# A graph kernel's edge scatters, moved: two ranges ahead of the first node tables, 22 beside the first convolution's count matrices, none beside the second's strips

## The chip, the cores and the metric

One core of one Trainium2 chip. The time is the device time of one launch in microseconds (us). Lower is better.

## The reference

Two layers over one graph of N = 6250 nodes (128 features) and E = 200000 edges; edges come sorted by destination, and the low destinations are far denser than the high ones.

```
h = relu(layernorm(x)); x = x + conv(relu(conv(h, W1, b1)), W2, b2)      # conv: segment_sum(h[src] * norm, dst)
h = relu(layernorm(x)); msg = relu(concat(h[src], edge_attr) @ W1 + b1)  # one message per edge
agg = segment_sum(msg, dst) / max(count, 1)
x = x + relu(concat(h, agg) @ W2 + b2)
```

## The kernel before, in words

Five engines run their own instruction streams: PE (TensorE), DVE (VectorE), ACT (ScalarE), POOL (GpSimd) and SP (SyncE). They meet at semaphores only. All loops of the stages below are written out, but for the message stage's.

1. **Setup.** DVE and PE rank the edges of 24 ranges (`RANGES`, each 32 columns of 128 edges): `slot_of_edge` says where each edge's row of 34 words goes, so that a range comes out sorted by source. POOL gathers, among other things, the 21 blocks of edges (L715) from which the first convolution's counts are built.
2. **Node tables.** For each of 13 groups of nodes the four compute engines make the table of `h @ W` and its three bf16 parts.
3. **First convolution.** The matrix of edge counts (source by target) is built in 24 strips of 256 targets. A strip has 32 windows: DVE makes one-hots for 8 visits at a time (L1753, L1757), PE multiplies them (`build_window`, L908), ACT takes the counts out of PSUM (L1206, semaphore `C["evacuated"]`) and stores the strip to DRAM. Between windows PE applies the strip before: 49 blocks by 3 parts, 147 matmuls of 256 columns (`apply`, L920). Strips 0 to 9 have windows with many visits, 10 to 15 have two visits of 392 columns, 16 to 23 two of 196.
4. **Node tables of the second convolution**, and then its 24 strips: the counts come back from DRAM (3136 KB a strip, two buffers), PE applies them with 147 matmuls a strip, and DVE adds the sum to `agg` (`add_strip`, L1766, semaphore `strip_added`).
5. **Third tables and messages.** The scattered rows (`permuted`) are loaded in order and joined with gathered rows, until the end of the run.

A few edges past the strips (one turn: 32 gathers on POOL, L638) are handled inside each convolution, on PE after strip 2's first segment and after strip 4.

The change is about POOL's 768 scatters. `scatter(r, pace)` issues the 32 indirect DMAs of range r; each writes 128 rows of 136 bytes. Halfway through a range it waits until the one before has landed and stages the next range's rows. The `pace` hook waits ahead of each scatter. `beside_windows(i)` lets scatter i go when ACT has taken out i * 768 / (number of scatters) windows; `beside_strips(i)` lets it go when a given strip has been added. Nothing needs the scattered rows before stage 5, and no engine waits for POOL there before that. POOL executes in order, so whatever stands behind a scatter on POOL waits for it: in stage 3 the turn's gathers stand ahead of the scatters, in stage 4 as well.

Of the kernel before, what the change touches and what calls it, by code (L numbers as in the profile page):

```python
# [13 lines left out]
P = 128  # L14
# [9 lines left out]
TC = 4  # L24
CE = TC * P
SLOTS = 8
# [15 lines left out]
STRIPS = 24  # L42
# [4 lines left out]
UNIT = 8  # L47
# [14 lines left out]
RANGES = 24  # L62
RT = 32
# [21 lines left out]
MESSAGE_CHUNKS = (PAIRS - 1) * PAIR_CHUNKS + LAST_CHUNKS  # L85
PAIR_STEPS = PAIR_UNITS + 2
PREPARED_AT = (5, DU + 8)
PACED = (16, 8)
KEYS = W * SB


# [18 lines left out]
assert DT % (SLOTS * TC) == 0 and LAST_CHUNKS % SLOTS == 0 and RANGES % 2 == 0 and DU % 2 == 0 and sum(UNIT_TILES) == SB and RT % 2 == 0  # L110
assert DT * P >= RANGE_ROWS
assert all((b - a) * SB <= 512 for a, b in TILE_GROUPS) and RT * P < OWN_EDGE and RANGES % RANK_BATCH == 0
assert sum(PACED) == RANGES and P % UNIT == 0


def build(nc, t, out):
    with ExitStack() as ctx:
# [300 lines left out]
        def tables_stored(engine, n):  # L418

            for q in range(2):  # L420
                engine.wait_ge(tab_stored[q], 16 * ((NG + 1 - q) // 2) * (n + 1))
# [206 lines left out]
        def _(pool):  # L628
            def gather_turn(e, n, i, pace=lambda k: None):
                for h in range(2):  # L630
                    pool.wait_ge(e["idx_" + "ab"[h]], i * 16 + 16)
                    for k in range(HALF * TC):
                        s, j = h * HALF + k // TC, k % TC
                        if j == 0:
                            pool.wait_ge(e["added"], i * SLOTS + s + 1)
                            pool.sem_inc(held["pool"])
                        pace(h * HALF * TC + k)
                        nc.gpsimd.indirect_dma_start(  # L638
                            rows[:, s, j * D:(j + 1) * D], None, tables[n],
                            bass.IndirectOffsetOnAxis(ap=idx[:, h, k:k + 1], axis=0),  # L640
                        ).then_inc(e["gathered"][s // e["apart"]], 16)

            def gather(e, n, first, turns):
                with pool.Fori(first, turns) as i:
                    gather_turn(e, n, i)
# [21 lines left out]
            def stage(r):  # L667
                pool.dma_start(edge_rows_of[:, r % 2], t["edge_cols"][:, r * RT:(r + 1) * RT].rearrange("p t c -> p (t c)")
                               ).then_inc(rows_staged[r % 2], 16)

            def scatter(r, pace=lambda k: None):

                pool.wait_ge(ranked, r + 1)
                pool.wait_ge(rows_staged[r % 2], 16 * (r // 2 + 1))
                for k in range(RT):
                    if k == RT // 2 and 1 <= r < RANGES - 1:
                        pool.wait_ge(scattered[(r - 1) % 2], ((r - 1) // 2 + 1) * RT * 16)
                        stage(r + 1)
                    pace(k)
                    nc.gpsimd.indirect_dma_start(  # L680
                        permuted, bass.IndirectOffsetOnAxis(ap=slot_of_edge[:, r * RT + k:r * RT + k + 1], axis=0),
                        edge_rows_of[:, r % 2, k * ROW_WORDS:(k + 1) * ROW_WORDS], None,
                    ).then_inc(scattered[r % 2], 16)

            def beside_windows(i):

                pool.wait_ge(C["evacuated"], BANKS + i * NW // (PACED[0] * RT))

            def beside_strips(i):

                strip = i * STRIPS // (SLOTS * TC + PACED[1] * RT)
                pool.wait_ge(strip_added[strip % 2], STRIPS // 2 + strip // 2 + 1)
                pool.sem_inc(held["pool"])

# [19 lines left out]
            for b in range(VB):  # L714
                nc.gpsimd.indirect_dma_start(  # L715
                    visit_edges[:, b].rearrange("p k e -> p (k e)"), None, t["edge_rows"],
                    bass.IndirectOffsetOnAxis(ap=visit_row[:, b:b + 1], axis=0)).then_inc(visits_gathered, 16)
            pool.wait_ge(blanked, 16 * (RANGES + 1))
            for n in range(2):
                tables_stored(pool, n)  # L720
                pool.wait_ge(G["own"], NG * (n + 1))
                pool.wait_ge(G["part"], NG * PARTS * (n + 1))
                e = shared_passes[n]
                if n == 0:
                    pool.wait_ge(edges_read, 2)
                    turns = pool.value_load(turns_i[0:1, 1:2], min_val=1, max_val=TURNS)
                    gather_turn(e, n, 0)
                    for r in range(PACED[0]):
                        scatter(r, lambda k: beside_windows(r * RT + k))
                    with pool.If(turns > 1):  # L730
                        gather(e, n, 1, turns)
                    pool.wait_ge(flag_ready, 2)
                    flagged = pool.value_load(flag[0:1, 0:1], min_val=0, max_val=1)
                else:
                    with pool.If(flagged < 1):
                        turns = pool.value_load(turns_i[0:1, 1:2], min_val=1, max_val=TURNS)
                        gather_turn(e, n, 0, beside_strips)
                        for r in range(PACED[0], RANGES):
                            scatter(r, lambda k: beside_strips(SLOTS * TC + (r - PACED[0]) * RT + k))
                        with pool.If(turns > 1):  # L740
                            gather(e, n, 1, turns)
                with pool.If(flagged > 0):
                    gather(full_passes[n], n, 0, TURNS)
                    if n:
                        for r in range(PACED[0], RANGES):
                            scatter(r)
            tables_stored(pool, 2)
            with pool.If(flagged < 1):
                gather_messages()
# [601 lines left out]
        def _(dve):  # L1351
# [335 lines left out]
            def edge_turn(e, i, first, messages=False):  # L1687

                bases = [None] * SLOTS
                if not e["every"]:  # L1690

                    _, bases = nc.values_load_multi_w_load_instructions(
                        chunk_window[0:1, 0, bass.ds(turn_at(first, i) * SLOTS, SLOTS)], engines=[mybir.EngineType.DVE],
                        min_val=0, max_val=NP - P)
# [191 lines left out]
            def messages_mixed():  # L1886
# [56 lines left out]
                def pair_of(k, chunks, last):  # L1943
                    added = 0
                    for u in range(PAIR_STEPS):
                        c = chunk_of(u, chunks)
                        if u == DU + 2:
                            add_range(k, 0, added)
                        if u < PAIR_UNITS:
                            source(k, u)  # L1950
                        if c is not None and (not last or c + 1 < chunks):
                            hot(k, c + 1)
                        if 1 <= u <= PAIR_UNITS:
                            target(k, u - 1)
                        if c is not None:
                            if c % SLOTS == 0:
                                _, bases = nc.values_load_multi_w_load_instructions(
                                    chunk_window[0:1, 0, bass.ds(k * PAIR_CHUNKS + (FIRST_TURN * SLOTS + c), SLOTS)],
                                    engines=[mybir.EngineType.DVE], min_val=0, max_val=NP - P)
                            add(k, c, bases[c % SLOTS])  # L1960
                            added = c + 1
                            if not last or c + 2 < chunks:
                                products_in(k, c + 2)
                        if u == PREPARED_AT[0]:
                            prepare(k, 1)
                        if u == PREPARED_AT[1] and not last:
                            dve.wait_ge(B["target"], k * PAIR_UNITS + DU)
                            prepare(k + 1, 0)
                    add_range(k, 1, added)
# [90 lines left out]
```

## Time and profile before

| | before |
|---|---|
| time, median of 3 runs | 3475.75 us (3471.35 to 3476.24) |
| span of the profiled execution | 3499.7 us |
| PE busy (matmul) | 2746.7 us, 78% |
| DVE busy | 1592.3 us, 45% |
| ACT busy | 1071.7 us, 31% |
| POOL busy | 1876.6 us, 54% |
| POOL scatters (L680) | 768, 871.7 us, 1135 ns each |
| queue 8, kind "instruction" | 103 packets, 1.69 MB |

The page gives the profiled execution's span alone, from the first to the last instruction; it is 24 us above the median of the runs shown. Busy time is time in which an engine executes; waits and the issuing of DMAs by SP and ACT are not in it. An indirect DMA on POOL counts as busy for as long as POOL works on its descriptors.

### The profile page before, as it was taken

Reading aid. Unit: us, or ns where it says so; the run is one execution under the profiler, and the core shown is the slowest. Engines: PE = TensorE matmul, PEld = TensorE weight load, DVE = VectorE, ACT = ScalarE, POOL = GpSimd, SP = SyncE. Lnnn points to the kernel's source line nnn. Section 1 sums busy time; section 2 is a strip of 40 time slices with the busy share of each in tenths; the row PEclk is TensorE's granted clock in tenths of the full one; section 3 lists DMA queues with packets and bytes.
Section 4 is the critical chain, followed back from the end, with each engine's and each line's share of the span. In section 5 each row is a group of like instructions: output and inputs, shape, how many; then the busy total and the mean of one; then the engine's idle time right before and its main releaser. Section 6 shows DMA issues by size and latency. Waiting matters only on the chain.

```text
span 3499.7 us, 54147 instructions
## 1 busy us (share of the span) xinstructions
PE 2746.7 (78%) x18926; PEld 2159.2 (62%) x18927; DVE 1592.3 (45%) x3094; ACT 1071.7 (31%) x3149; POOL 1876.6 (54%) x1751
## 2 busy tenths in 40 slices
PE   2755697889947765787878647998998989888987
PEld 0114486777736654565656536777777777777766
DVE  7988985766623433000000253444444444444436
ACT  6504234556625533000000012333333333333321
POOL 3750767778866732534445134565565555555660
PEclk9995989999968977878888768999999999999989
DMA  9012122323322323433434232323233233332321
GB/s 358 28 35 76 34 83 96 130 98 128 147 85 94 133 97 97 159 124 132 163 125 163 91 98 69 94 90 101 90 95 92 86 104 92 89 92 88 105 73 45
DMA packets 127284, 365.86 MB, mean 105 GB/s; under 512 B 36226, under 2 KB 79591, under 8 KB 120599
## 3 DMA queue, kind: packets, MB, share of 16 engines
q10 hardware_dynamic: 21792, 186.56, 13.8%
q0 software_dynamic: 58928, 89.45, 10.0%
q1 hardware_dynamic: 46377, 87.47, 7.1%
q8 instruction: 103, 1.69, 0.2%
q14 instruction: 84, 0.69, 0.1%
HBM read 230.80 MB, written 132.55 MB: 104 GB/s over the span
## 4 chain that ended last, share of the span: by engine, by line
PE 62%; DVE 11%; issue 10%; another core or an unknown queue 8%; ACT 3%; POOL 2%; DMA 1%; ACTq 1%; DVEq 0%; SPq 0%; POOLq 0%
PE ps_feat L920 12%; PE ps_node L920 11%; PE ps_extra L1069 7%; PE ps_sum L1032 4%; PE pre_banks L908 3%; PE pre_banks L1023 3%; PE ps_feat L1057 3%; PE ps_feat L1053 3%; PE ps_sum L1053 2%; PE ps_sum L1057 2%; PE ps_node L1053 2%; PE ps_node L1057 2%; POOL region_b L705 2%; DVE region_c L1757 2%
## 5 line engine op out<-in xcount | busy, mean ns | idle before, releaser
L680 POOL DMA_INDIRECT permuted<-rows_or_lows,slot_of_edge x768 | 871.7, 1135 | 528.3 <-DVE agg L1766 222.9
L662 POOL DMA_INDIRECT rows<-table,region_a x800 | 786.5, 983 | 685.7 <-issue 210.5
L920 PE MATMUL ps_feat<-region_a,region_b 128*128 128x256 bf16 x3528 | 506.9, 290 | 71.4 <-issue 70.8
L920 PE MATMUL ps_node<-region_a,region_b 128*128 128x256 bf16 x3528 | 513.6, 290 | 60.6 <-issue 57.6
L920 PEld LDWEIGHTS ps_feat<-region_a,region_b 128*128 128x128 bf16 x3528 | 359.3, 103 | 156.5 <-issue 97.4
L920 PEld LDWEIGHTS ps_node<-region_a,region_b 128*128 128x128 bf16 x3528 | 358.2, 103 | 148.7 <-issue 86.9
L1069 PE MATMUL ps_extra<-region_b 128*128 128x128 f32 x2352 | 335.0, 284 | 86.4 <-ACT region_b L1299 48.0
L1069 PEld LDWEIGHTS ps_extra<-region_b 128*128 128x128 f32 x2352 | 302.0, 199 | 92.6 <-issue 72.1
L1757 DVE TENSOR_TENSOR region_c<-iota_key,region_c 128x1568 bf16<-128x1568 f16 (+1 forms) x324 | 353.2, 1090 | 0.0
L1933 DVE TENSOR_TENSOR region_b<-consts,region_a 128x512 f32<-128x512 f32 x336 | 208.2, 620 | 186.9 <-PE ps_extra L1069 97.6
L1928 DVE TENSOR_SCALAR region_b<-rows_or_lows,consts 128x512 f32<-128x512 bf16 x336 | 159.8, 479 | 288.8 <-remote 133.1
L1206 ACT ACTIVATE region_a<-pre_banks 128x392 bf16<-128x392 f32 x384 | 190.7, 499 | 283.2 <-PE pre_banks L908 172.1
L1032 PE MATMUL ps_sum<-onehot,rows 128*128 128x64 f32 x1600 | 216.6, 279 | 14.0 <-issue 13.8
L1032 PEld LDWEIGHTS ps_sum<-onehot,rows 128*128 128x128 f32 x1600 | 211.7, 204 | 21.2 <-issue 20.1
L1146 ACT ACTIVATE std<-moments,eps 128x4 f32<-128x4 f32 x26 | 7.7, 297 | 654.7 <-DVE moments L1589 654.4
L1766 DVE TENSOR_TENSOR agg<-agg,ps_node 128x256 f32<-128x256 f32 x24 | 10.1, 421 | 408.6 <-PE ps_node L920 322.0
L1766 DVE TENSOR_TENSOR agg<-agg,ps_feat 128x256 f32<-128x256 f32 x24 | 10.1, 421 | 392.6 <-PE ps_feat L920 325.1
L638 POOL DMA_INDIRECT rows<-table,idx x64 | 67.8, 1059 | 210.6 <-DVEq L1743 95.4
L1912 DVE TENSOR_TENSOR agg<-agg,ps_sum 128x64 f32 x200 | 43.8, 219 | 273.5 <-PE ps_sum L1032 133.4
L908 PE MATMUL pre_banks<-region_c,rows_or_lows 128*128 128x196 bf16 (+1 forms) x678 | 117.2, 278 | 62.0 <-ACT region_a L1206 34.0
L1753 DVE TENSOR_TENSOR rows_or_lows<-iota_units,region_c 128x1024 bf16<-128x1024 bf16 x162 | 111.3, 687 | 115.4 <-PE pre_banks L908 34.9
L908 PE MATMUL pre_banks<-region_c 128*128 128x196 bf16 (+1 forms) x644 | 112.1, 278 | 49.9 <-DVE region_c L1757 23.7
(263 smaller groups left out, 4534.9 us busy)
## 6 DMA issues: line engine op xcount, KB each, us to landing
counts<-region_a ACTq DMA_DIRECT2D x24, 3136.0 KB
region_a<-counts ACTq DMA_DIRECT2D x22, 3136.0 KB
rows_or_lows<-block_lows ACTq DMA_DIRECT2D x72, 448.0 KB
permuted<-region_b SPq DMA_DIRECT2D x25, 833.0 KB
region_a<-permuted SPq DMA_DIRECT2D x24, 833.0 KB
rows_or_lows<-edge_cols_in POOLq DMA_DIRECT2D x24, 544.0 KB
region_a<-attr_t_in SPq DMA_DIRECT2D x50, 256.0 KB
rows<-table,region_a POOLq DMA_INDIRECT x800
```

The source lines that it names most:

```text
L662: nc.gpsimd.indirect_dma_start(rows[:, s, j * D:(j + 1) * D], None, tables[2], bass.IndirectOffsetOnAxis(ap=message_rows[:, c * TC + j:c * ...
L680: nc.gpsimd.indirect_dma_start(permuted, bass.IndirectOffsetOnAxis(ap=slot_of_edge[:, r * RT + k:r * RT + k + 1], axis=0), edge_rows_of[:, ...
L908: ins = mm(bank[:, part * n:part * n + n], hot_source(u)[:, :, j], hot_key(u)[:, j // SIDE, 0:n, j % SIDE], start=(k == 0), stop=(k == SPL ...
L920: ins = mm(strip_bank(buf), parts[:, h, k], counts[buf][:, h], start=(h == 0 and k == 0), stop=(h == SB - 1 and k == PARTS - 1), skip_grou ...
L1032: last = mm(ps_sum[0][:, 0:CW], rows[:, c % SLOTS, j * D:(j + 1) * D], onehot[:, c % 2, j, 0:CW], start=(j == 0), stop=(j == TC - 1))
L1053: mm(banks[u % 3][:, 0:n * D], attr_turned[u % 2][0:n * DE, :], edge_w[0:n * DE, 0:n].rearrange("p j d -> p (j d)"), start=True, stop=Fals ...
L1057: last = mm(banks[u % 3][:, j * D:(j + 1) * D], source_hot[u % 2][:, j * P:(j + 1) * P], messages_of[:, b0 + j], start=False, stop=(j == n ...
L1069: last = mm(ps_extra[:, 0:P], block_msgs[u % 2][:, j * D:(j + 1) * D], target_hot[u % 2][:, j * P:(j + 1) * P], start=(u % DU == 0 and j = ...
L1206: nc.scalar.activation(counts[strip % 2][:, :, at:at + W], count_banks[w % BANKS][:, 0:KEYS].rearrange("p (d h) -> p h d", h=SB), ACT.Copy ...
L1757: v.tensor_tensor(hot_key(u)[:, :, 0:n], iota_key[:, None, 0:n].to_broadcast([P, UNIT // SIDE, n, SIDE]), keys[:, :, None, :].to_broadcast ...
L1928: v.tensor_scalar(source_hot[u % 2][:, 0:n], lows, partition, None, ALU.is_equal).then_inc(B["source"], 1)
L1933: v.tensor_tensor(target_hot[u % 2][:, 0:n * P].rearrange("p (j n) -> p j n", n=P), iota[:, None, :].to_broadcast([P, n, P]), block_dst[u ...
```

## The change

`EARLY_RANGES = 2`: ranges 0 and 1 are scattered without pace right after the 21 gathers of stage 1, ahead of POOL's wait for the first tables. Ranges 2 to 23 are paced by the windows of the first convolution, so 704 scatters go over the same 768 windows where 512 did. The 256 scatters beside the second convolution's strips are gone, and the pace of its 32 gathers is now 16 * 32 = 512 steps over 24 strips, not 288. The branches for inputs that the fast path refuses (`flagged`) are not taken here.

```
-PACED = (16, 8)
+EARLY_RANGES = 2
+PACED = (RANGES - EARLY_RANGES, 0)
...
-                strip = i * STRIPS // (SLOTS * TC + PACED[1] * RT)
+                strip = i * STRIPS // (16 * SLOTS * TC)
...
             pool.wait_ge(blanked, 16 * (RANGES + 1))
+            for r in range(EARLY_RANGES):
+                scatter(r)
             for n in range(2):
                 tables_stored(pool, n)
...
                     gather_turn(e, n, 0)
-                    for r in range(PACED[0]):
-                        scatter(r, lambda k: beside_windows(r * RT + k))
+                    for r in range(EARLY_RANGES, RANGES):
+                        scatter(r, lambda k: beside_windows((r - EARLY_RANGES) * RT + k))
...
                         gather_turn(e, n, 0, beside_strips)
-                        for r in range(PACED[0], RANGES):
-                            scatter(r, lambda k: beside_strips(SLOTS * TC + (r - PACED[0]) * RT + k))
```

POOL's stream at the end of stage 1, before; L715 are the gathers of the edge blocks, L726 reads a register once the first tables are stored, L638 is the first gather of the turn:

```order
L715 DMA region_a<-edge_rows_in,visit_row 128x256 [waits visit_rows_ready]
L715 DMA region_a<-edge_rows_in,visit_row 128x256 x20
L726 TENSOR_LOAD turns_i [waits node_own,node_part,tab_stored_1,edges_read,tab_stored_0,blanked]
L726 ISA x2
L638 DMA rows<-table,idx 128x128 [waits idx_a_shared_0,added_shared_0]
```

The same place in the changed kernel, whose lines are numbered one to three higher (L716 is L715, L681 is L680, L729 is L726):

```order
L716 DMA region_a<-edge_rows_in,visit_row 128x256 [waits visit_rows_ready]
L716 DMA region_a<-edge_rows_in,visit_row 128x256 x20
L681 DMA permuted<-rows_or_lows,slot_of_edge 248832x34 [waits rows_staged_0,ranked,blanked]
L681 DMA permuted<-rows_or_lows,slot_of_edge 248832x34 x31
L681 DMA permuted<-rows_or_lows,slot_of_edge 248832x34 [waits rows_staged_1,ranked]
L681 DMA permuted<-rows_or_lows,slot_of_edge 248832x34 x15
L669 DMA rows_or_lows<-edge_cols_in 128x1088 [waits scattered_0]
L681 DMA permuted<-rows_or_lows,slot_of_edge 248832x34 x16
L729 TENSOR_LOAD turns_i [waits node_part,node_own,edges_read,tab_stored_1,tab_stored_0]
L729 ISA x2
```

64 scatters now follow the gathers at once, and none of their waits is for the tables. The second place is POOL's stream in the second convolution, before, from the turn's last gathers on:

```order
L638 DMA rows<-table,idx 128x128 [waits added_shared_1,strip_added_0]
L638 DMA rows<-table,idx 128x128 [waits strip_added_0] x3
L680 DMA permuted<-rows_or_lows,slot_of_edge 248832x34 [waits strip_added_0,ranked,rows_staged_0]
L680 DMA permuted<-rows_or_lows,slot_of_edge 248832x34 [waits strip_added_0] x3
L680 DMA permuted<-rows_or_lows,slot_of_edge 248832x34 [waits strip_added_1] x12
L668 DMA rows_or_lows<-edge_cols_in 128x1088 [waits scattered_1]
L680 DMA permuted<-rows_or_lows,slot_of_edge 248832x34 [waits strip_added_0] x12
```

All of the L680 and L668 rows from there on are gone in the changed kernel; 12 scatters a strip stood here.

## Rows read from the trace of the kernel before

In windows the columns are: the stretch and its length in us; busy us (and instructions) of PE, PE's weight loads, DVE, ACT and POOL; PE's granted clock (1 is full), the DMA engines' share, GB/s. In timelines they are: start, length, engine, line and operation, and in brackets the idle time before it and what ended it.

**Rows 1.** Windows by stage, all engines: strips 0-2, 3-9, 10-15, 16, 17-23; second convolution

```profile
356.80:528.00 171.20, 135.54 (x1154) 119.11 (x1155) 154.16 (x217) 56.06 (x192) 121.66 (x85) 0.92 0.19 59
528.00:789.60 261.60, 218.73 (x1926) 191.22 (x1925) 176.01 (x232) 130.17 (x448) 194.22 (x165) 0.92 0.30 108
789.60:959.80 170.20, 166.00 (x1269) 134.01 (x1268) 116.93 (x103) 112.95 (x384) 139.42 (x105) 0.99 0.36 135
959.80:1035.60 75.80, 31.34 (x223) 23.34 (x221) 12.80 (x18) 18.01 (x64) 52.93 (x53) 0.68 0.21 73
1035.60:1270.60 235.00, 181.21 (x1469) 149.46 (x1468) 89.32 (x119) 122.03 (x448) 162.55 (x153) 0.87 0.32 116
...
1352.70:1979.00 626.30, 490.94 (x3592) 378.14 (x3592) 14.40 (x40) 0.00 (x0) 280.68 (x295) 0.82 0.37 135
```

**Rows 2.** The same windows, scatters of L680 alone: POOL busy (x), clock, DMA

```profile
356.80:528.00 171.20, 83.62 (x52) 0.92 0.19 59
528.00:789.60 261.60, 191.34 (x160) 0.92 0.30 108
789.60:959.80 170.20, 137.68 (x102) 0.99 0.36 135
959.80:1035.60 75.80, 52.34 (x52) 0.68 0.21 73
1035.60:1270.60 235.00, 159.67 (x148) 0.87 0.32 116
```

**Rows 3.** What ended POOL's idle time before its scatters, us and times

```profile
  ACT region_a L1206: 124.4, 159
```

**Rows 4.** Timeline, one strip of the second convolution: PE, and POOL's first and last scatter

```profile
1446.67 9.77 PE L920 MATMUL ps_feat<-region_a,region_b 128*128 128x256 bf16 x88
...
1465.25 6.75 PE L920 MATMUL ps_feat<-region_a,region_b 128*128 128x256 bf16 x45 [1.03 <-issue]
...
1448.11 0.98 POOL L680 DMA_INDIRECT permuted<-rows_or_lows,slot_of_edge  x1 [10.74 <-DVE agg L1766]
...
1462.04 0.96 POOL L680 DMA_INDIRECT permuted<-rows_or_lows,slot_of_edge  x1 [0.31 <-issue]
```

**Rows 5.** DMA queues in 1465 to 1468 us

```profile
q8 instruction: 1, 0.02, 2.5%
```

**Rows 6.** Timeline: the turn's place after strip 4, strip 5, POOL's pause, and strip 23

```profile
1490.41 7.37 PE L920 MATMUL ps_node<-region_a,region_b 128*128 128x256 bf16 x41 [0.34 <-issue]
...
1518.82 18.42 PE L920 MATMUL ps_feat<-region_a,region_b 128*128 128x256 bf16 x147
...
1538.52 0.96 POOL L680 DMA_INDIRECT permuted<-rows_or_lows,slot_of_edge  x1 [23.61 <-DVE agg L1766]
...
1962.59 16.21 PE L920 MATMUL ps_feat<-region_a,region_b 128*128 128x256 bf16 x147
```

**Rows 7.** Timeline, strips 0 and 1 of the second convolution: first gather, PE, strip 2

```profile
1362.35 0.98 POOL L638 DMA_INDIRECT rows<-table,idx  x1 [91.00 <-DMA idx<-src_t_in]
...
1396.32 11.01 PE L920 MATMUL ps_feat<-region_a,region_b 128*128 128x256 bf16 x81 [0.30 <-issue]
...
1420.48 9.77 PE L920 MATMUL ps_node<-region_a,region_b 128*128 128x256 bf16 x88
```

**Rows 8.** Timeline, first node tables: POOL's gathers, ACT, and POOL's next work

```profile
235.39 0.94 POOL L715 DMA_INDIRECT region_a<-edge_rows_in,visit_row  x1 [31.28 <-DVE visit_row L1575]
...
260.47 0.94 POOL L715 DMA_INDIRECT region_a<-edge_rows_in,visit_row  x1 [0.30 <-issue]
...
356.85 0.95 POOL L638 DMA_INDIRECT rows<-table,idx  x1 [95.43 <-DVEq L1743]
...
265.14 0.60 ACT L1172 ACTIVATE agg<-ps_feat 128x512 f32<-128x512 f32 x1 [18.59 <-remote]
```

**Rows 9.** Timeline, strip 16 of the first convolution: ACT and POOL around POOL's pause

```profile
1016.96 0.50 ACT L1206 ACTIVATE region_a<-pre_banks 128x392 bf16<-128x392 f32 x1 [15.57 <-remote]
...
1017.82 0.96 POOL L680 DMA_INDIRECT permuted<-rows_or_lows,slot_of_edge  x1 [4.08 <-ACT region_a L1206]
```

More of the change, by code:

```diff
@@ L112 @@
 assert all((b - a) * SB <= 512 for a, b in TILE_GROUPS) and RT * P < OWN_EDGE and RANGES % RANK_BATCH == 0
-assert sum(PACED) == RANGES and P % UNIT == 0
+assert EARLY_RANGES + sum(PACED) == RANGES and P % UNIT == 0
 def build(nc, t, out):
@@ L743, in _ @@
                     gather(full_passes[n], n, 0, TURNS)
-                    if n:
-                        for r in range(PACED[0], RANGES):
-                            scatter(r)
             tables_stored(pool, 2)
```

## The prediction

> **What bounds the kernel now.** I read the windows by stage first, then the timeline of single strips in both convolutions, then the same for the first node tables. The stages up to 1979 us are the only ones that the change touches; the messages behind them move as a block. In the second convolution the busy shares mislead. PE looks like the bound, 491 of 626.3 us [rows 1], but one strip is 147 matmuls, and strip 23 did them in 16.21 us and strip 5 in 18.42 [rows 6], while a strip takes 25 on average. The timeline of a usual strip shows where the rest goes [rows 4]: PE runs 88 matmuls in 9.77 us, then for 8.8 us it executes a matmul here and there, waiting for nothing that the profile shows ("issue"), then 45 more run from 1465.25. POOL's 12 scatters of that strip (288 paced steps over 24 strips) go from 1448.11 to 1463.0, one each 1.26 us (0.96 busy and 0.30 between). PE resumes 2.2 us after the last of them, and the packet of queue 8, kind "instruction", lands in just that stretch [rows 5]. Strip 5 is the counter-example: POOL had paused for 23.61 us and PE ran all 147 without a gap [rows 6]. At the start of the convolution 24 gathers do the same as scatters, and PE gets going again at 1396.32 [rows 7]; no counts are loaded then, so the loads are not needed for it.
>
> My reading: while POOL issues indirect DMAs back to back at 1.26 us, the other engines' instructions hardly arrive. They live on what they hold for some 9 us and then stand, until POOL pauses. It is seen with ACT too. In the first node tables it waits 18.59 us for something "remote" and goes on 3.7 us after POOL's 21 gathers end [rows 8]. In strip 16 ACT stands 15.57 us, and when it goes on POOL has been idle for 3 us (its scatter at 1017.82 ends a pause of 4.08, held by ACT) [rows 9]. POOL had stopped because the windows, which need ACT, had not come on. That is a loop: POOL starves the windows, catches up with them, is held by its pace, and lets them run.
>
> The Trainium skill, in Runtime: NRT & Kernel Launch, section Instruction fetch mechanics, says that instructions are streamed in 16 KiB blocks over a DMA queue of the engine's own and that this is mostly hidden. The block size agrees with the page (1.69 MB in 103 packets); "hidden" does not agree with the gap, and what would follow if the gap had another cause is rival 3.
>
> **Removed: 256 scatters beside the second strips.** Strip 0 takes 18 us as now. Strip 1 still meets the turn's gathers. Before, 24 went at once and 8 more with strip 2; now the pace lets all 32 go at 1362, 40 us long, so PE resumes some 10 us later than 1396, but the 8 and the first 4 scatters no longer follow, which cost it about as much. I leave strips 0 and 1 at their 68 us (1352.7 to 1420.5 [rows 1, 7]). The other 22 strips cost 16.2 us each [rows 6]: 356 us. The turn's work after strip 4 stays at 21 us (1497.8 to 1518.8 [rows 6]). 68 + 356 + 21 = 445 against 626: **-181 us**. Bounds: at strip 5's 18.2 us a strip it is -137; if strip 1 comes out shorter by what 8 issues cost (0.69 us each, worked out below), -187. The counts' loads become the next thing to be late, but their share of the DMA engines' time, at most 0.37 * 626.3 / 22 = 10.5 us a strip [rows 1], is under the 16 us that they would have.
>
> **Added: 64 scatters ahead of the tables.** POOL has nothing to do from 261 to 356.85, 95.43 us [rows 8], and 64 * 1.26 = 81 us fit, so POOL itself is not late. But 21 gathers (26 us) made a burst after which ACT had stood 18.6 us [rows 8]. The burst becomes 107 us, without a pause: its one inner wait is for range 0's landing, 16 scatters (20 us) old by then. ACT would stand until 346 where it now goes on at 265, and DVE and PE hang on it in each group of nodes. I take **+75 us**, six less than 81 for what trickles through. Bounds: 64 * 0.69 = 44, and 81; 0.69 is the price of a scatter beside a strip now: 22 strips take 626.3 - 68 - 21 = 537 us, 24.4 each, so 8.2 us more than 16.2 for 12 scatters.
>
> **Added: 192 scatters beside the windows.** A strip was due 512 / 24 = 21.3, now 704 / 24 = 29.3. Here two groups are read together [rows 1, 2]. Strips 10 to 15 run at 28.4 us, PE 98% busy, with POOL at it without a break: 102 scatters in 170.2 us, 1.67 each, because DVE is busy and each takes 1.35 (137.68 / 102). At that pace nobody starves, but 128 were due. At 959.8 POOL had done 314 of 341. Strip 16, where DVE has half the work, pays: 52 scatters in 75.8 us, against 33.6 us for strips 17 to 23. So 31 more scatters than a strip's 21 cost 42 us, 1.36 us each. That is the marginal price: once POOL is behind, each further scatter is issued while the others stand. Now add up what the changed kernel must do. Strips 0 to 2 are held by DVE (154 of 171 us busy [rows 1]), and POOL is held there too; I let them absorb 24 of the 36 more that are due (to 76). Strips 3 to 9 then need 217 instead of 160: 57 more. Strips 10 to 15 absorb none and end 74 behind. Strip 16 must do 103 instead of 52: 51 more. Strips 17 to 23: 205 for 148: 57 more. 165 * 1.26 = 208 us. POOL is held by ACT's windows for 124.4 us in all [rows 3], part of which is the pause that the others need; I let 25 us of it be used: **+183 us**. Bounds: all 124.4 us usable, of which the 24 absorbed above already take 30, 208 - 94 = +114; and 192 at 1.36, +261.
>
> The Trainium skill speaks against this part in SBUF — State Buffer, section SBUF: two separate sides: a VectorE instruction in a two-port mode locks GpSimd out, and descriptors of its DMAs wait. The trace fits it (1.35 us for 0.96 [rows 2, 4]). By that rule alone 192 scatters more would cost POOL 192 * 0.39 = 75 us and PE nothing, since the same page lets PE and ACT wait for nobody; this is close to rival 1.
>
> **Sum.** -181 + 75 + 183 = +77 us. The changes are made in the profiled execution, 24 us longer than the median of the runs; I carry the difference over to the median: 3475.75 + 77 = **3553 us**, 2.2% slower.
>
> **Rivals.**
> 1. *POOL's held time is slack* (0.17; faster). The pause that a catch-up needs is short, and 99 of the 192 scatters (124.4 / 1.26) go where POOL is held now. The other 93 and the 64 early ones cost the 0.69 us that one costs beside a strip: 64 + 44 - 181 = -73, **3403 us**. For it: in strips 10 to 15 POOL ran for 170 us and nobody starved. Against it: the 1.36 us of strip 16, and that each hold of POOL is the time in which the windows get on. It decides once the windows' part costs under about 106 us (181 - 75) or, with the early ones at 44, under 137.
> 2. *The early scatters are free* (0.07). POOL is idle there, and ACT's 18.59 us come from the 131 KB that each of the 21 gathers moves, where a scatter moves 17 KB. Then 183 - 181 = +2: **3478 us**. Against it: in strip 16 scatters alone stopped ACT.
> 3. *The gap in the second strips comes from the loads of the counts*, which start with each strip as the scatters do (0.05). Nothing is gained there: 75 + 183 = +258, **3734 us**. Against it: the gathers at 1362, before any load, and the resumption 2.2 us after the last scatter.
> 4. *As forecast, also if POOL never catches up* (0.71). If POOL ends the first convolution some 100 scatters behind, they run on into the next stage at 0.69 us instead of 1.26: 57 us less, 3496. Its own range is 3490 to 3630.
>
> **How the numbers follow.** A measurement tells 0.2%, 7 us. The range 3420 to 3640 holds nearly all of rival 4 and of rival 2 and part of rival 1; outside are rival 3 and half of rival 1, with the tails of the forecast. Faster: rival 1 and bits of 2 and 4, 0.21. Same: 0.05. Slower: 0.74.
>
> **What would show it.** Second convolution: strips at 16 us, clock near 1, no "issue" gaps after strip 1; 25 us strips would mean rival 3. Node tables: ACT's "remote" wait grows from 19 to some 95 us and the first L638 gather comes at about 430 instead of 356.85; if it comes by 365, rival 2. First convolution: strips 10 to 15 still 28.4 us, strip 16 about 140 us (75.8 + 51 * 1.26), strips 3 to 9 and 17 to 23 about 10 us longer each; if POOL's held time falls to near zero and the strips keep their length, rival 1. The forecast is most exposed in the marginal price: it comes from one strip.

## The result, and the profile after

The changed kernel takes 3627.72 us (median of 4 runs, 3612.63 to 3636.14) against 3475.99 us of the kernel before (4 runs, 3471.35 to 3505.18); the ratio worked out over all runs is 1.0418, with an interval of 1.0373 to 1.0464. It is slower, as forecast, and by more than the 2.2% of the forecast. The profiled executions span 3610.8 and 3499.7 us, 111 us apart, and every sum below is made against these 111. The medians are 152 us apart: the before's profile is of a longer execution than its median, the changed kernel's of a shorter one.

The page of the changed kernel, busy time and instruction queue:

```profile
PE 2715.0 (75%) x18926; PEld 2151.8 (60%) x18927; DVE 1598.7 (44%) x3094; ACT 1069.7 (30%) x3149; POOL 1859.3 (51%) x1751
q8 instruction: 103, 1.69, 0.2%
```

No engine has notably more to do than before (the most is DVE, by 6 us). The windows by stage, all engines: strips 0-2, 3-9, 10-15, 16, 17-23, and the second convolution.

```profile
435.60:623.60 188.00, 142.70 (x1161) 117.33 (x1161) 155.71 (x218) 55.55 (x192) 137.38 (x119) 0.94 0.22 65
623.60:941.90 318.30, 241.34 (x1919) 193.10 (x1918) 177.65 (x232) 128.77 (x448) 238.71 (x212) 0.88 0.27 93
941.90:1113.50 171.60, 166.12 (x1269) 133.91 (x1268) 117.14 (x103) 112.38 (x384) 140.52 (x106) 0.99 0.36 131
1113.50:1266.00 152.50, 36.43 (x215) 24.53 (x213) 12.82 (x18) 18.47 (x64) 108.00 (x112) 0.56 0.16 47
1266.00:1581.80 315.80, 202.66 (x1475) 160.30 (x1472) 89.35 (x120) 123.31 (x445) 216.87 (x212) 0.77 0.26 93
...
1662.40:2106.40 444.00, 408.58 (x3592) 361.23 (x3592) 14.76 (x40) 0.00 (x0) 30.26 (x32) 0.94 0.45 172
```

The same windows, scatters of L681 alone:

```profile
435.60:623.60 188.00, 98.24 (x84) 0.94 0.22 65
623.60:941.90 318.30, 235.26 (x206) 0.88 0.27 93
941.90:1113.50 171.60, 138.78 (x103) 0.99 0.36 131
1113.50:1266.00 152.50, 105.70 (x108) 0.56 0.16 47
1266.00:1581.80 315.80, 214.01 (x207) 0.77 0.26 93
```

Against [rows 1, 2] the stages differ by: first node tables +79 (the first gather starts at 435.63 instead of 356.85), strips 0 to 2 +17, strips 3 to 9 +57, strips 10 to 15 +1, strip 16 +77, strips 17 to 23 +81, second convolution -182. That is +129 (the terms are rounded). The first convolution as a whole, to its last sum, is 234 us longer. The second tables (-3) and the messages behind (-16), which the change doesn't touch, make up most of what is left to 111.

ACT in the first node tables, and POOL's next gather; idle time in brackets:

```profile
270.91 0.60 ACT L1170 ACTIVATE agg<-ps_feat 128x512 f32<-128x512 f32 x1 [24.11 <-remote]
282.02 0.60 ACT L1154 ACTIVATE rows<-ps_turn 128x512 f32<-128x512 f32 x1 [9.99 <-remote]
315.04 0.60 ACT L1170 ACTIVATE agg<-ps_extra 128x512 f32<-128x512 f32 x1 [31.20 <-remote]
326.15 0.60 ACT L1154 ACTIVATE rows<-pre_banks 128x512 f32<-128x512 f32 x1 [10.00 <-remote]
354.96 0.60 ACT L1170 ACTIVATE agg<-ps_feat 128x512 f32<-128x512 f32 x1 [26.99 <-remote]
...
435.63 0.98 POOL L639 DMA_INDIRECT rows<-table,idx  x1 [91.43 <-DVEq L1741]
```

One wait of 18.59 us [rows 8] has become five of 102 us together. POOL's scatters were held by ACT for:

```profile
  ACT region_a L1204: 119.7, 141
```

against 124.4 us [rows 3]: nearly all of it is still there.

Strips 1 to 3 of the second convolution on PE, first and last of the turn's gathers, and a late strip:

```profile
1679.85 0.72 PE L918 MATMUL ps_feat<-region_a,region_b 128*128 128x256 bf16 x5
...
1693.74 0.37 PE L918 MATMUL ps_feat<-region_a,region_b 128*128 128x256 bf16 x1 [1.73 <-issue]
...
1717.58 16.38 PE L918 MATMUL ps_feat<-region_a,region_b 128*128 128x256 bf16 x123 [1.04 <-issue]
1733.79 16.21 PE L918 MATMUL ps_node<-region_a,region_b 128*128 128x256 bf16 x147
...
1672.36 0.98 POOL L639 DMA_INDIRECT rows<-table,idx  x1 [92.86 <-DMA idx<-src_t_in]
...
1711.11 0.94 POOL L639 DMA_INDIRECT rows<-table,idx  x1 [0.30 <-issue]
...
1961.35 16.21 PE L918 MATMUL ps_feat<-region_a,region_b 128*128 128x256 bf16 x147
```

While the 32 gathers go, one each 1.25 us, PE executes single matmuls, most of them 1.4 to 3.5 us apart. Some 6 us after the last gather it runs whole strips, and from then on each takes 16.05 us, but for strip 5 behind the turn (35 us). PE is not alone in standing: it is done with strip 0 at 1680.01, and DVE adds that sum only when the stretch is over:

```profile
1717.74 0.42 DVE L1764 TENSOR_TENSOR agg<-agg,ps_node 128x256 f32<-128x256 f32 x1 [56.47 <-remote]
```

In the queues there is no packet of queue 8 from 1672 to 1717.5 us, and one from 1717 to 1720. It starts at 1718.72, when PE has been running at full pace for 1.1 us:

```profile
q8 instruction: 1, 0.02, 1.9%
```

### The profile page after: what moved, and what is told of

It reads as the page before. It is cut to its first block, busy times and chain, and to the rows that moved or that the text cites. A ratio compares the mean times of both kernels' runs of the same rounds, so it can differ in the third digit from the quotient of the medians.

```text
span 3610.8 us, 53890 instructions
## 1 busy us (share of the span) xinstructions
PE 2715.0 (75%) x18926; PEld 2151.8 (60%) x18927; DVE 1598.7 (44%) x3094; ACT 1069.7 (30%) x3149; POOL 1859.3 (51%) x1751
## 4 chain that ended last, share of the span: by engine, by line
PE 57%; another core or an unknown queue 15%; DVE 10%; issue 8%; ACT 4%; POOL 2%; DMA 2%; ACTq 1%; DVEq 0%; SPq 0%
PE ps_feat L918 10%; PE ps_node L918 9%; PE ps_extra L1067 7%; PE ps_sum L1030 4%; PE pre_banks L906 4%; PE pre_banks L1021 3%; PE ps_node L1051 2%; PE ps_node L1055 2%; PE ps_sum L1051 2%; PE ps_feat L1055 2%; PE ps_sum L1055 2%; PE ps_feat L1051 2%; POOL region_b L706 2%; ACT region_a L1204 2%
## 5 line engine op out<-in xcount | busy, mean ns | idle before, releaser
L681 POOL DMA_INDIRECT permuted<-rows_or_lows,slot_of_edge x768 | 854.5, 1113 | 312.4 <-issue 192.7
L918 PE MATMUL ps_feat<-region_a,region_b 128*128 128x256 bf16 x3528 | 486.8, 286 | 47.5 <-issue 38.6
L918 PE MATMUL ps_node<-region_a,region_b 128*128 128x256 bf16 x3528 | 484.6, 283 | 10.7 <-issue 7.9
L1751 DVE TENSOR_TENSOR region_c<-iota_units,region_c 128x1024 bf16<-128x1024 bf16 x162 | 111.7, 690 | 112.4 <-remote 51.0
L1204 ACT ACTIVATE region_a<-ps_turn 128x392 bf16<-128x392 f32 x192 | 95.5, 498 | 220.9 <-remote 106.4
```

Source lines behind the costliest of these rows:

```text
L681: nc.gpsimd.indirect_dma_start(permuted, bass.IndirectOffsetOnAxis(ap=slot_of_edge[:, r * RT + k:r * RT + k + 1], axis=0), edge_rows_of[:, ...
L918: ins = mm(strip_bank(buf), parts[:, h, k], counts[buf][:, h], start=(h == 0 and k == 0), stop=(h == SB - 1 and k == PARTS - 1), skip_grou ...
L1204: nc.scalar.activation(counts[strip % 2][:, :, at:at + W], count_banks[w % BANKS][:, 0:KEYS].rearrange("p (d h) -> p h d", h=SB), ACT.Copy ...
L1751: v.tensor_tensor(hot_source(u), iota_units[:], visit_lo[:, None, u * UNIT:(u + 1) * UNIT].to_broadcast([P, P, UNIT]), ALU.is_equal)
```

## Experiments

Twelve runs, in five batches; two of them repeat a kernel. The batches turned out to be of two kinds, and this matters more than any edit. In the first the kernel before takes 3493.82 us (13 runs), much as in the result (3475.99); in the other four it takes 2825.0 to 2826.8 us. I call the first kind *starving* and the second *quiet*; the names stand for the times and for engines that stand still beside POOL's DMAs, not for a cause. The listed number of the chip is 1, 0, 6, 4 and again 1, so the kind doesn't go with the number; whether it belongs to the chip, to the machine around it or to the occasion isn't known. A ratio is always to the kernel before in the same batch.

### The starving batch

**early_alone**: only the first part of the change.

```
+EARLY_RANGES = 2
-PACED = (16, 8)
+PACED = (14, 8)
```

The loop of scatters beside the second strips and its pace stay as in the kernel before.

> The kernel before, but with ranges 0 and 1 scattered ahead of the first tables (the change's first part alone): 14 ranges beside the windows, 8 beside the second strips as before. Marginal price (mine): the tables end 79 us later, as in the changed kernel; 64 scatters fewer beside the windows give back about 8 us in strips 0 to 2 and 1.3 us each on some 50 others, in all about 75. Sum about +5: 3465 to 3500. Average price (rival: a scatter costs the 0.7 us of the second strips wherever it stands): 79 - 45 = +34, 3510. Early scatters free (rival): 3390 to 3410.

Measured: 3486.35 us, 0.9998 [0.9948, 1.0049]. The first tables take the same 79 us more, and the first convolution ends at 1290.97 us where it ended at 1288.48: 64 scatters fewer beside the windows give back 76 us, 1.19 each. The average price of a scatter there is far lower (next kernel), so it is the marginal price that counts. The rival of the expectation, an average price of 0.7 us, would have given 3510, and free early scatters 3400.

**no_scatters**: the 768 scatters are left out, and so the permuted edge rows that the messages read are never written.

```
-                    nc.gpsimd.indirect_dma_start(
-                        permuted, bass.IndirectOffsetOnAxis(ap=slot_of_edge[:, r * RT + k:r * RT + k + 1], axis=0),
...
-                    ).then_inc(scattered[r % 2], 16)
+                    pool.sem_inc(scattered[r % 2], 16)
```

> The kernel before without any scatter (this leaves the rows of edges unwritten; the semaphore is raised by hand, everything else is issued). If back-to-back indirect DMAs on POOL starve the other engines: the second convolution takes 444 us as in the changed kernel, strips 3 to 9 and 17 to 23 of the first take 21 to 27 us each instead of 33 to 37, strip 16 no more than its neighbours, the first convolution about 700 to 740 us instead of 932, the whole 3060 to 3120. If the windows are bound by VectorE or the counts' stores instead: the first convolution stays above 880 and the whole above 3250.

Measured: 3107.53 us, 0.8911 [0.883, 0.8991] (2 runs). Strips 3 to 9 take 29.3 us, 10 to 15 28.3, 17 to 23 22.5, the second strips 16.05. I had expected 3060 to 3120 in all, and 21 to 27 us for strips 3 to 9, which is 2 us too low:

```profile
1303.00 16.21 PE L917 MATMUL ps_node<-region_a,region_b 128*128 128x256 bf16 x147
```

The first convolution ends 192 us earlier than in the kernel before, so its 512 scatters cost 0.37 us each on average, though the last ones cost 1.2. The loads of the counts are all there and leave PE alone: rival 3 is out.

**landed2**: a scatter waits until the one two before it has landed.

```
+                    if k >= 2:
+                        pool.wait_ge(scattered[r % 2 * 2 + k % 2], (r // 2 * RT + k) // 2 * 16)
...
-                    ).then_inc(scattered[r % 2], 16)
+                    ).then_inc(scattered[r % 2 * 2 + k % 2], 16)
```

The waits of POOL, SP and ACT for whole ranges are changed to the four semaphores that this needs.

**filler**: two small memsets on POOL behind each scatter, each waited for, so that where nothing else holds POOL a scatter is issued every 2.2 us and not every 1.26.

```
+                    for _ in range(2):
+                        filled[0] += 1
+                        nc.gpsimd.memset(iota_x[:, NB:P], 0.0).then_inc(full_passes[0]["idx_a"], 1)
+                        pool.wait_ge(full_passes[0]["idx_a"], filled[0])
```

> The kernel before with one wait more: each scatter waits until the one two before it has landed, so at most two are in flight. All the work is done. If it is the unbroken burst that starves the others (mine): the scatters come at 1.5 us or slower, the gaps of the second strips go (16 to 18 us a strip), strip 16 falls to under 50 us, the whole is 3200 to 3330. If each scatter costs the others its 0.7 to 1.3 us however it is spaced (rival): no gain or a loss, 3470 to 3560, since POOL falls further behind.

> The kernel before with two small memsets on POOL (128 x 76, each waited for) after each scatter: spacing by POOL's own work, nothing limits the DMAs in flight. If the spacing of the descriptor work is what counts (mine): as landed2, or nearer to before if the two memsets take under 0.2 us. If what counts is that earlier scatters have landed (the DMA queue's backlog): this one gains less than landed2 at the same spacing. If neither counts: 3470 to 3600.

Measured: landed2 3589.39 us, 1.0268 [1.0173, 1.0363]; filler 3590.62, 1.0282 [1.0199, 1.0365]. I had expected 3200 to 3330. Both are slower than the kernel before, and yet in filler every strip of both convolutions but one runs as if there were no scatters at all. Its first convolution ends at 1097.52 us (no_scatters: 1096.75). In the second, PE runs whole strips beside scatters 2.2 us apart:

```profile
1709.43 16.21 PE L926 MATMUL ps_node<-region_a,region_b 128*128 128x256 bf16 x147
...
1709.70 0.96 POOL L682 DMA_INDIRECT permuted<-rows_or_lows,slot_of_edge  x1 [0.84 <-POOL iota_x L688]
...
1711.90 0.97 POOL L682 DMA_INDIRECT permuted<-rows_or_lows,slot_of_edge  x1 [0.84 <-POOL iota_x L688]
```

The same number of scatters, of the same bytes, to the same rows; what differs is the spacing, made by two small memsets. The loss is POOL's lag, in two places. The sum of strip 4 comes at 1241.23, that of strip 5 at 1613.35: the turn behind strip 4 needs 32 gathers, and on POOL these stand behind all scatters of the first 16 ranges, for which POOL is now too slow. Even so the second convolution ends 77 us earlier than in the kernel before (1902.20 against 1978.83). Then the last scatters, until 2147.93, hold back the gathers of the messages: the first is issued at 2153.29 us, in the kernel before at 2063.50. These 90 us are nearly all of the loss. landed2 waits 417 us at strip 5. It also shows where the limit lies: POOL issued seven scatters 1.26 us apart, since those before had landed in time, and PE stuttered; then one took 8 us to land, POOL paused for 6.00 us, and in that pause PE got going.

```profile
1713.54 0.96 POOL L684 DMA_INDIRECT permuted<-rows_or_lows,slot_of_edge  x1 [0.30 <-issue]
1714.59 0.27 PE L924 MATMUL ps_node<-region_a,region_b 128*128 128x256 bf16 x1 [0.46 <-issue]
...
1717.45 11.96 PE L924 MATMUL ps_node<-region_a,region_b 128*128 128x256 bf16 x108 [0.41 <-issue]
1721.85 0.96 POOL L684 DMA_INDIRECT permuted<-rows_or_lows,slot_of_edge  x1 [6.00 <-DMA permuted<-rows_or_lows,slot_of_edge]
```

Its last strip takes 97 us, from 1975.37 to 2072.01. POOL catches up there with 68 scatters, nearly all 1.26 us apart, and PE stutters to the end of them. Early in it, in 1980 to 1990, a packet of queue 8 arrives, and PE stutters on for another 75 us:

```profile
q8 instruction: 1, 0.02, 0.8%
...
2056.36 0.37 PE L924 MATMUL ps_feat<-region_a,region_b 128*128 128x256 bf16 x1 [2.43 <-issue]
2059.16 0.37 PE L924 MATMUL ps_feat<-region_a,region_b 128*128 128x256 bf16 x1 [2.43 <-issue]
```

### The quiet batches

The next kernels were written to combine spacing with an order in which the gathers don't come late. All of them ran in quiet batches.

**order_only**: 3 ranges early, 12 beside the windows, 9 beside the second strips, no memsets.

```
-EARLY_RANGES = 2
-PACED = (RANGES - EARLY_RANGES, 0)
+EARLY_RANGES = 3
+PACED = (12, 9)
```

The loop beside the second strips is back, as in the kernel before.

> 3 ranges early, 12 beside the windows, 9 beside the second strips, no spacing: the control for the two spaced kernels. By the marginal prices: 96 early at 1.23 = +118, 128 fewer beside the windows at 1.33 = -170, 32 more beside the strips at 0.69 = +22 against the kernel before, so about 3450. Second strips at 25 us as before. Rival, the order by itself is what matters: 3300 or less.

Measured: 2822.89 us (8 runs), 0.9985 [0.9975, 0.9996]. The 3450 that I had expected belong to the starving kind. Here PE runs 147 matmuls in 16.21 us right beside scatters 1.26 us apart, which stopped it in the kernel before [rows 4]:

```profile
1304.19 16.21 PE L923 MATMUL ps_feat<-region_a,region_b 128*128 128x256 bf16 x147
...
1304.60 0.96 POOL L681 DMA_INDIRECT permuted<-rows_or_lows,slot_of_edge  x1 [0.30 <-issue]
1305.86 0.96 POOL L681 DMA_INDIRECT permuted<-rows_or_lows,slot_of_edge  x1 [0.30 <-issue]
1307.13 0.96 POOL L681 DMA_INDIRECT permuted<-rows_or_lows,slot_of_edge  x1 [0.30 <-issue]
```

The turn's 32 gathers go from 1148.89 us on, 1.25 us apart as in the changed kernel's profile above. PE works on beside them (360 matmuls in 1148 to 1187), and its instruction queue with it; in 1165 to 1175:

```profile
q8 instruction: 1, 0.02, 0.7%
```

The whole queue carries as many packets and bytes as in the starving profiles, in the same share of the span:

```profile
q8 instruction: 103, 1.69, 0.2%
```

**spaced1** and **spaced_half**: the same order, with one memset (waited for) behind each scatter, or behind every second.

```
+                    for _ in range(1 if k % 2 == 1 else 0):
+                        filled[0] += 1
+                        nc.gpsimd.memset(iota_x[:, NB:P], 0.0).then_inc(full_passes[0]["idx_a"], 1)
+                        pool.wait_ge(full_passes[0]["idx_a"], filled[0])
```

> 3 ranges early, 12 beside the windows, 9 beside the second strips, and after each scatter a 128x76 memset that POOL waits for, so that scatters are issued some 1.7 us apart and not 1.26. The second turn's gathers stand behind 12 ranges instead of 16, so they should not be late. Theory (other engines' instructions do not arrive while POOL issues at 1.26 us, and they do when it leaves gaps): strips run as without any scatters, the first convolution ends some 10 to 30 us later than the 1097 us of the kernel without scatters, second strips take 16 us, the scatters end some 50 to 100 us after the second convolution: 3150 to 3300 us. Rival, the gap must be nearly as long as in the experiment with two memsets (2.2 us): strips of 20 us and more, 3400 or more. Rival, the scatters cost by number, whatever the spacing: no better than the control without memsets, 3450.

> As the kernel before it in this batch, with the memset after every second scatter only: 1.5 us on average, in pairs 1.26 apart. If the mean rate is what counts and the bound lies below 1.5 us: strips as without scatters, POOL done earlier, 3130 to 3250 us. If pairs at 1.26 still starve the others: strips of 20 to 24 us in the second convolution, 3350 to 3450.

Measured: 2974.06 us, 1.0512 [1.0494, 1.0529], and 2864.61, 1.0129 [1.0113, 1.0146]. The strips are those of order_only, but for strip 1 of the first convolution in spaced1 (78 us, not 49); the loss is POOL's time. The first message gather starts at 1629.2 us in order_only, 1671.7 in spaced_half and 1804.5 in spaced1, since scatters are still to be done. What this spacing does for starved engines stays unseen. **spaced_half2** was the same kernel in a later batch:

> The kernel with a memset after every second scatter once more, in case it meets a chip on which the others starve. There: if a mean of 1.5 us between issues is enough, the first convolution ends by about 1110 us, second strips take 16 us and the whole about 3150 us, well under the kernel before's 3480; if pairs at 1.26 us still starve the others, strips of 20 us and more and 3350 or more. On a chip without starvation it repeats 1.013 of before.

Quiet again: 2862.95 us, 1.0129 [1.0112, 1.0146], a repetition and nothing more.

**no_early**: the changed kernel with all 24 ranges beside the windows.

```
-EARLY_RANGES = 2
+EARLY_RANGES = 0
```

> The changed kernel without its first part: all 24 ranges are scattered beside the windows, none ahead of the node tables, none beside the strips. My theory (a scatter costs the time that it takes to issue, 1.3 us, wherever POOL issues without a pause): the 79 us of the early ones come back and 64 more beside the windows cost 64 * 1.33 = 85, so about 3634 us, the changed kernel's time within 15. Rival, each further scatter beside the windows is dearer than the last (1.37 in the last strips, 1.6 for these): about 3650. Rival, POOL does not catch up by the end of the first convolution, and what is left falls into the second node tables and costs less: about 3600.

Measured, quiet batch: 3110.12 us, 1.1002 [1.0984, 1.1021]; the 3634 expected were again a price of the starving kind. No strip is lengthened. The sum of strip 5 of the second convolution comes 321.7 us after that of strip 4, in order_only 35.3 us: PE waits for the gathers, which stand behind 768 scatters.

**after_again**: the changed kernel, unaltered.

> The changed kernel itself once more, because the last batch ran on a chip on which nobody starves (the kernel before takes 2827 us there and the strips run beside scatters at 1.26 us as without them). If it meets such a chip: 704 scatters beside the windows do not fit into the first convolution, the second turn's gathers stand behind what is left on POOL, and PE waits for them at strip 4; that is the kernel without early scatters less 64 * 1.26 = 81 us: about 3029 us, 1.072 of before. If it meets a chip like the first one: 1.04 of before. Rival: on such a chip the early scatters cost time after all, and it comes to 3110.

Measured, quiet batch: 3048.33 us (2 runs), 1.0794 [1.0768, 1.082]. So the change makes the kernel slower on this kind too, by 223 us, and for another reason. POOL's last scatter and the first gather behind it, and who waited for whom:

```profile
1411.30 0.96 POOL L681 DMA_INDIRECT permuted<-rows_or_lows,slot_of_edge  x1 [0.30 <-issue]
1412.56 0.98 POOL L639 DMA_INDIRECT rows<-table,idx  x1 [0.30 <-issue]
```

```profile
PEld ps_sum L869 <- DMA rows<-table,idx: 224.7, 4, 201.0
```

(us in total, number of waits, the longest.)

I had expected 3029 us. The last scatter is issued at 1411.30 us, 332 us after the first convolution is over (1079.10), and the gathers follow it at once. Strip 5 comes 256.4 us after strip 4; less order_only's 35.3 that is 221, the whole of the 223. The early scatters keep POOL busy 22 us longer (its first gather starts at 362.1 us, in no_early at 340.3), but no strip comes later for it: the first sum is at 456.1 us in both. Those 22 us account for most of why no_early and this kernel lie 62 us apart and not the 81 that I had worked out.

**spaced_all**: spaced_half, with a memset behind every second gather of the messages too.

```
                             bass.IndirectOffsetOnAxis(ap=message_rows[:, c * TC + j:c * TC + j + 1], axis=0),
                         ).then_inc(e["gathered"][s], 16)
+                        space(j)
```

> 3 ranges early, 12 beside the windows, 9 beside the strips, a memset that POOL waits for after every second scatter, and after every second gather of the messages too. On a chip where the others starve: if a mean of 1.5 us between issues is enough, strips of 29.3, 28.3, 22.5 and 16.05 us, the second convolution over by about 1600 us, and messages shorter than their 1505 us by up to the 265 us that they are shorter on the other chip: 2850 to 3150 us. If pairs at 1.26 still starve: 3350 and more. On the chip without starvation: nothing to gain, the memsets cost POOL time in the messages, 2870 to 2950 us.

Measured, quiet batch: 3036.61 us, 1.0754 [1.0734, 1.0774]. I had expected 2870 to 2950. The second convolution ends at 1543.8 us (order_only 1545.1), and against spaced_half the kernel is 172 us slower: that is what the memsets cost the messages. Where nobody starves, spacing those gathers is a loss.

**robust**: 3 ranges early, 13 beside the windows, 8 beside the strips, a memset behind every second scatter.

> 3 ranges early, 13 beside the windows, 8 beside the second strips, a memset after every second scatter. Against the same with 12 and 9 the scatters of one range (52 us at 1.62) move into the first convolution, where POOL was idle for 70 us at the end; so the scatters should end before the tables of the messages do. On a chip without starvation: the 38 us that the spacing cost are gone, 2820 to 2835 us, the same as before. On a chip where the others starve: first convolution over by about 1110 us, second strips at 16 us, 3100 to 3150 us against 3480 of before; if pairs at 1.26 us still starve, 3350 and more.

Measured, quiet batch: 2823.31 us (10 runs), 0.9986 [0.9957, 1.0016]. There it costs nothing against the kernel before, and by the ratios it is 7% better than the changed one (0.9986 against 1.0794). Whether it helps where the others stand still was not seen, so no version here is shown to beat the kernel before.

## Why the prediction was right, and where it was off

The forecast (slower, 3553) held in sign, and its range (3420 to 3640) held the time, with 12 us to spare. The growth was twice the forecast: 152 us between the medians for 77. Its steps, in order:

- **The second convolution, -181.** Measured -182. Strips 0 and 1 took 72 us (68 forecast), the turn 19 (21), the other strips 16.05 each (16.2). Right, and no_scatters rules out the loads (rival 3).
- **The early scatters, +75.** Measured +79, 1.23 us each. Rival 2 fails here: ACT stands for 102 us while 17 KB scatters are issued. It holds in a quiet batch.
- **The windows, +183.** Measured +234. This is the term that was mis-sized, in two of its parts. The 25 us of held time that I let be used weren't: POOL is held for 119.7 us now and was for 124.4. And I let strips 0 to 2 absorb 24 scatters; they took 32 more and became 17 us longer. Without both the working is simple: 192 scatters at 1.22 us are 234. The price of 1.26 that I read off one strip was nearly right: 1.23 (64 early), 1.19 (64 taken out of the windows by early_alone), 1.22. Strip 16 became 152.5 us where I had said 140, by 56 scatters at 1.37. Strips 10 to 15 absorbed none, as said.
- **Rival 1**, that POOL's held time is slack, falls with the same 119.7 us. The pause is what the windows need to get on. One reading stands behind both: the total of POOL's pauses was fixed by what the others had to do in them, so a scatter more simply comes on top. In the second convolution a scatter had cost 182 / 256 = 0.71 us, in the windows and the tables 1.2. The change moved 256 scatters from the cheap place to the dear one.
- **Rival 4** (POOL ends behind): the scatters end at 1578.5 us, before the last sum of the first convolution at 1600.98. They were not late.
- **What no term had.** The second tables (-3 us) and the messages (-16 us), which the change doesn't touch, were shorter in the changed kernel's profile. That is luck for the forecast: it hides part of the 51 us by which the windows were mis-sized.
- **The mechanism.** In the starving batch it is the spacing of POOL's indirect DMAs that makes the others stand. filler changes that and adds only two memsets, and all strips but the waiting strip 5 are whole; no_scatters shows the same by leaving them out. The prediction went one step further: the others' instructions hardly arrive. The runs do not show that, and for PE they speak against it. [rows 5] was read the wrong way round: its packet starts at 1467.90 us, and PE had resumed at 1465.25. Queue 8 keeps step with PE in every run: counted in PE's own instructions, the 29 packets of the second convolution start within 20 instructions of the same place in the kernel before and in no_scatters, and there are some 256 from one packet to the next. So a packet comes late because PE is late. Nor does one that has come help. In the kernel before one arrives from 1771.70 us on, and PE stutters for the 8 us right behind it, until 2 us after POOL's scatters end:

```profile
q8 instruction: 1, 0.02, 1.6%
...
1764.82 7.15 PE L920 MATMUL ps_feat<-region_a,region_b 128*128 128x256 bf16 x64
...
1772.15 0.38 PE L920 MATMUL ps_feat<-region_a,region_b 128*128 128x256 bf16 x2 [0.18 <-issue]
...
1779.95 0.37 PE L920 MATMUL ps_feat<-region_a,region_b 128*128 128x256 bf16 x1 [1.03 <-issue]
1780.65 4.66 PE L920 MATMUL ps_feat<-region_a,region_b 128*128 128x256 bf16 x21 [0.34 <-issue]
```

  The packet in landed2's last strip says the same. The other instruction queue, 14, goes with POOL's program (84 packets in the kernel before, 81 in the changed one, 100 in filler); for ACT and DVE no view shows one. The Trainium skill (Runtime: NRT & Kernel Launch, section Instruction fetch mechanics) calls instruction fetch mostly hidden. No trace here speaks against that for PE, in batches of either kind. The forecast did not need the step: its prices were read from strips, whatever makes the others stand.
- **What the prediction had no case for** is the other kind of run. Every price in it is one of a starving run. In a quiet one the terms are 0 for the second strips, 0 for the early scatters and 0 for the strips beside windows, plus a wait of 221 us for gathers queued behind 704 scatters. I had read that POOL lags and asked only what a lag of scatters costs, not what stands behind them in POOL's queue. That "slower" is right for the quiet kind too is luck. In the starving run that wait is hidden, because starving makes the first convolution so long (to 1600.98 us, where the quiet one ends at 1079.10) that POOL is through in time.

**Open.** What holds the other engines in a starving run, and what differs between the two kinds. It is neither the number nor the place of the instruction packets: queue 8 has 103 packets and 0.2% in both, within 64 of PE's instructions at the same place in the second convolution of order_only as of the kernel before, and the gathers and scatters are issued at the same 1.25 and 1.26 us. No view here shows more. Nor is the spacing known at which the starving ends: 1.26 us starves, 2.2 doesn't, and in strips 10 to 15, where DVE slows POOL, 1.67 doesn't [rows 2].

## What to carry to other kernels

Before work is moved to an idle-looking engine, price the next unit and not the average one: here 0.37 us on average and 1.2 at the margin. Then read what stands behind the moved work in the same queue; both kinds of run made this change slower, one by starving the others and one by 32 gathers queued behind 704 scatters. And where a gap says only "issue" on several engines at once, look for the engine whose pause ends it. A packet of the instruction queue near the gap proves nothing until you have asked which came first, the packet or the resumption.

## What the runs showed of the hardware

- The same program takes 3475.99 us in one batch and 2825 us in another, and most executions of a batch lie within 1% of its median. Even the messages, which no edit touched, differ: from the last sum of the second convolution to the end it is 1509 us in no_scatters (starving) and 1277 in order_only (quiet).
- While it starves, PE is not stopped altogether: it executes a single matmul of 0.37 us every 1 to 4 us (1693.74 above). In the gathers of the changed kernel nearly all single matmuls start 1.4, 2.1, 2.8 or 3.5 us apart, multiples of 0.70 us.
- A spacing of 2.2 us made by two idle memsets gives the other engines full speed in the starving batch. A limit of two scatters in flight doesn't quite: second strips of 14 to 24 us where filler has 16.05, and 97 us for the last.
